# A Flamingo block on one core: row tables, means and gathers around the choice of experts

## What is computed

```
x = x + tanh(g_xattn[0]) * cross_attention(layernorm(x), ctx)         # 77 keys
x = x + tanh(g_ffn[0])   * quantised_gated_ffn(layernorm(x))
x = x + tanh(g_xattn[1]) * attention_16_heads(layernorm(x), ctx)
x = x + tanh(g_ffn[1])   * experts(layernorm(x))

def experts(x):                                   # 2048 tokens
    logits = (x @ w_red) @ (wg / norm(wg)).T      # 8 experts
    gates = softmax(logits);  idx = argmax(gates);  score = max(gates)
    h = gelu(x @ W1[idx] + b1[idx])               # 256 -> 512
    return (h @ W2[idx] + b2[idx]) * score        # 512 -> 256
```

## Time and profile before

| | us |
|---|---|
| median of 3 runs | 446.13 (445.56 to 446.71) |
| the profiled execution | 443.87 |
| its span | 442.1 |
| PE, DVE, ACT, POOL busy | 402.4, 314.8, 252.8, 133.8 |
| mean granted clock of TensorE | 0.947 of 2.4 GHz |

### The profile page before, as it was taken

The page is one execution under the profiler, slowest core; times in us unless marked ns, Lnnn a source line. Parts: engine busy times, 40 slices in busy tenths (PEclk is TensorE's granted clock), DMA queues, the critical chain, the costliest instruction groups (busy, mean ns, idle before and its releaser), DMA issues.

```text
span 442.1 us, 8460 instructions
## 1 busy us (share of the span) xinstructions
PE 402.4 (91%) x2922; PEld 305.0 (69%) x2923; DVE 314.8 (71%) x662; ACT 252.8 (57%) x423; POOL 133.8 (30%) x159
## 2 busy tenths in 40 slices
PE   8998899999997906999999999999996999999992
PEld 7887744444444606888886777777685589999991
DVE  3999985449999998886487799988876344444442
ACT  3563556559999893551358777887832433443320
POOL 6614145200000072231119700020127745552221
PEclk9999999999999555999999999999999799999997
DMA  7920000000002000500049920002221847666600
GB/s 245 307 5 0 1 3 0 0 0 0 0 0 64 2 0 0 116 0 0 1 154 394 397 12 3 2 1 98 93 76 54 292 150 215 208 211 171 170 22 0
DMA packets 37813, 38.34 MB, mean 87 GB/s; under 512 B 16620, under 2 KB 28595, under 8 KB 37524
## 3 DMA queue, kind: packets, MB, share of 16 engines
q1 hardware_dynamic: 35571, 32.76, 24.3%
q0 software_dynamic: 2208, 5.14, 3.5%
HBM read 33.66 MB, written 5.15 MB: 88 GB/s over the span
## 4 chain that ended last, share of the span: by engine, by line
PE 65%; DVE 9%; ACT 6%; POOL 3%; issue 3%; DMA 2%; DVEq 0%; ACTq 0%; POOLq 0%
PE quad L1760 30%; PE bank L1760 27%; PE bank L2083 4%; ACT tmp L965 2%; ACT big_u L960 1%; DMA big_u<-token_rows,k_blockdiag 1%; ACT big_u L812 1%; DVE amZ L1356 1%; DVE amU L1362 1%; DVE mx L1578 1%; PE bank L2120 1%; DVE big_g L1576 1%; PE quad L1804 1%; POOL big_g L782 1%; POOL big_u L782 1%
## 5 line engine op out<-in xcount | busy, mean ns | idle before, releaser
L1760 PE MATMUL quad<-yT,ffn_w 128*128 (+1 forms) x128 | 56.3, 593 | 0.0
L812 ACT ACTIVATE big_u<-bank 77x512 f32<-77x512 f32 (+2 forms) x72 | 38.9, 589 | 11.8 <-PE bank L2083 10.6
L1760 PEld LDWEIGHTS quad<-yT,ffn_w 128*128 128x128 f32 x128 | 24.0, 190 | 29.5 <-issue 28.3
L1760 PE MATMUL bank<-big_u,yT 128*128 x184 | 43.6, 380 | 0.5 <-issue 0.5
L1760 PEld LDWEIGHTS quad<-yT,x_rows 128*128 128x128 f32 x336 | 40.7, 192 | 1.0
L1760 PE MATMUL quad<-yT,x_rows 128*128 128x128 f32 x336 | 40.9, 275 | 0.0
L789 POOL DMA_INDIRECT out<-yT,k_blockdiag x23 | 23.0, 1001 | 46.5 <-DVE yT L1728 45.7
L1760 PEld LDWEIGHTS bank<-big_u,yT 128*128 128x128 f32 x184 | 33.2, 190 | 4.7 <-issue 1.1
L1712 DVE TENSOR_TENSOR yT<-quad,tmp 128x512 f32<-128x512 f32 x21 | 14.5, 691 | 28.7 <-PE quad L1760 28.7
L812 ACT ACTIVATE yT<-quad 128x256 f32<-128x256 f32 x23 | 8.7, 382 | 40.3 <-PE quad L1804 40.2
L1760 PE MATMUL quad<-ffn_w,big_u 128*128 128x256 f32 x144 | 31.5, 380 | 0.1
(11 more groups left out here) (350 smaller groups left out, 913.3 us busy)
## 6 DMA issues: line engine op xcount, KB each, us to landing
x_rows<-in_L_ffn_W SPq DMA_DIRECT2D x21, 512.0 KB, 3.8
big_g<-in_L_ffn_W SPq DMA_DIRECT2D x1, 4096.0 KB, 14.5
big_u<-in_L_ffn_W SPq DMA_DIRECT2D x1, 4096.0 KB, 25.0
x_rows<-in_x SPq DMA_DIRECT2D x4, 512.0 KB, 6.5
ffn_w<-in_L_ffn_b SPq DMA_DIRECT2D x1, 2048.0 KB, 25.0
tmp<-bias_by_distance SPq DMA_DIRECT2D x2, 616.0 KB, 5.8
token_rows<-x_rows SPq DMA_DIRECT2D x1, 1032.0 KB, 5.4
tmp<-in_L_ffn_b SPq DMA_DIRECT2D x1, 1024.0 KB, 5.5
```

The costliest lines, as they stand in the source:

```text
L812: act.activation(out_, in_, ACT.Copy, **k).then_inc(done, 1)
L1760: return pe.matmul(out_, lhsT=lhsT, rhs=rhs, start=first, stop=last)
```

## The change

1. **Row tables.** AT_ROW is made ahead of PLACE, tile by tile: eleven tiles by VectorE with a tensor_scalar of 128 columns each, five by ScalarE as 1 - (place - rem)^2, cut at 0 (three squares and one difference, then two and one). PE waits for PLACE and all of VectorE's tables first.
2. **Small matmuls.** PE's counting of tiles 14 and 15 stands between the two halves of tile 14's projection. VectorE's counting moves ahead of the residual of tile 14, the residual of tile 15 behind two steps of the positions.
3. **Last rows.** The means of the last tiles are computed one by one, each on its own wait; the power is written straight into X, without the copy.
4. **Gathers.** AHEAD is 8 instead of 12, the groups are 1, 1, 2, 2, 2, 4, 4, 4 and 3.
5. **Idle matmuls.** 12 + 11 become 19 ahead of the placing matmuls, 16 become 18 behind them, three new ones stand between the transposes of the first two slots.
6. Four semaphores of VectorE become one that it raises four times.

```diff
-GATHERS = (1, 1, 2, 4, 4, 4, 4, 3)
-AHEAD = 12
+GATHERS = (1, 1, 2, 2, 2, 4, 4, 4, 3)
+AHEAD = 8
...
+        BY_DVE = 11
...
             def last_rows_ready(k):
                 b, e = ROW_PARTS[2 + k]
-                pool.wait_ge(s.x3_done, e)
-                pool.tensor_scalar(nmean[:, k, :], xsum[:, k, :], -1.0 / D, None, ALU.mult).then_inc(s.nmean_sb, 1)
+                for u in range(2):
+                    pool.wait_ge(s.x3_done, b + u + 1)
+                    pool.tensor_scalar(nmean[:, k, u:u + 1], xsum[:, k, u:u + 1], -1.0 / D, None,
+                                       ALU.mult).then_inc(s.nmean_sb, 1)
                 pool.wait_ge(s.dev_sb, 2 * k + 2)
                 c.link(pool.tensor_scalar(ve4[:, b:e], xdev[:, k, :], 1.0 / D, EPS, ALU.mult, ALU.add))
-                c.link(pool.tensor_tensor(rstd4[:, b:e], ve4[:, b:e], mhalf[:, b:e], ALU.pow))
-                pool.tensor_copy(X[:, b:e, RSTD], rstd4[:, b:e])
...
+                c.link(pool.tensor_tensor(X[:, b:e, RSTD], ve4[:, b:e], mhalf[:, b:e], ALU.pow))
...
             squares(1)
+            act.wait_ge(s.rem_sb, 1)
+            for n, (t, e) in enumerate(((BY_DVE, BY_DVE + 3), (BY_DVE + 3, NT))):
+                for u in range(e - t):
+                    ins = act.activation(apart[:, n, u, :], lane[:, :], ACT.Square, scale=-1.0, bias=rem[:, t + u:t + u + 1])
+                c.link(ins)
+                act.activation(AT_ROW[:, t:e, :], apart[:, n, 0:e - t, :], ACT.Relu, scale=-1.0,
+                               bias=ones[:, 0:1]).then_inc(s.at_row_a, 1)
             act.wait_ge(s.lxs_sb, 1)
...
+            for t in range(BY_DVE):
+                dve.tensor_scalar(AT_ROW[:, t, :], lane[:, :], rem[:, t:t + 1], None, ALU.is_equal).then_inc(s.at_row_sb, 1)
...
-            for g in range(NT // 4):
-                dve.tensor_tensor(AT_ROW[:, 4 * g:4 * g + 4, :], lane[:, :].unsqueeze(1).to_broadcast([P, 4, P]),
-                                  rem[:, 4 * g:4 * g + 4].unsqueeze(2).to_broadcast([P, 4, P]),
-                                  ALU.is_equal).then_inc(s.at_row_sb, 1)
...
-                project(t, 0)
-                counts(t, NT)
+                project(t, 0, lambda: counts(t, NT))
                 project(t, 1)
-                idle_work(pb[2], 12)
...
-            idle_work(pb[2], 11)
+            idle_work(pb[2], 19)
...
-            idle_work(pb[2], 16)
+            idle_work(pb[2], 18)
...
-            for u in range(2):
-                inputs(u, 0)
+            inputs(0, 0)
+            idle_work(pb[2], 3)
+            inputs(1, 0)
```

More of the change, by code:

```diff
@@ L178, in __init__ @@
         self.nmean_sb = sem("nmean_sb")
+        self.rem_sb = sem("rem_sb")
+        self.at_row_a = sem("at_row_a")
         self.dev_sb = sem("dev_sb")
@@ L436, in flamingo_kernel @@
         nmean = sb("x3_nmean", [P, 2, 2])
+        apart = part(TMP, 5632, [P, 2, 3, P], F16)
         LM = sb("lm", [P, NT])
@@ L1286, in _ @@
             dve.wait_ge(s.els_sb, 1)
-            dve.tensor_scalar(hscale[:, :], els[:, :], 4.0, HD ** -0.5, ALU.min, ALU.mult).then_inc(s.hsc_sb, 1)
+            dve.tensor_scalar(hscale[:, :], els[:, :], 4.0, HD ** -0.5, ALU.min, ALU.mult).then_inc(s.l1_prep_sb, 1)
             c.link(dve.tensor_tensor(wg2[:, :], wg[:, :], wg[:, :], ALU.mult))
@@ L1292, in _ @@
             dve.tensor_scalar(bo1c[:, :], bo1c[:, :], tg[:, 1:2], None, ALU.mult)
-            dve.tensor_scalar(bo1[:, :], bo1[:, :], tg[:, 1:2], None, ALU.mult).then_inc(s.wo_sb, 1)
+            dve.tensor_scalar(bo1[:, :], bo1[:, :], tg[:, 1:2], None, ALU.mult).then_inc(s.l1_prep_sb, 1)
             dve.wait_ge(s.wnorm_sb, 1)
@@ L1297, in _ @@
             c.link(dve.reciprocal(wss[:, 2:3], wss[:, 1:2]))
-            dve.tensor_scalar(wgn[:, :], wg[:, :], wss[:, 2:3], None, ALU.mult).then_inc(s.wgn_sb, 1)
+            dve.tensor_scalar(wgn[:, :], wg[:, :], wss[:, 2:3], None, ALU.mult).then_inc(s.l1_prep_sb, 1)
             dve.tensor_scalar(keepv[:, :], keepc8[:, :], -1.0, 1.0, ALU.mult, ALU.add)
@@ L1645, in _ @@
             gate(LAST, NT)
-            residual(LAST, 0)
             dve.wait_ge(s.cnt_ps, 1)
@@ L1653, in _ @@
             c.link(dve.tensor_reduce(start_e[:, :], earlier[:, :, :], AX.X, ALU.add))
-            residual(LAST, 1)
+            residual(LAST, 0)
             c.link(dve.scalar_tensor_tensor(CUM, start_e[:, :].unsqueeze(1).to_broadcast([P, NT, E]), float(P),
@@ L1658, in _ @@
             c.link(dve.tensor_tensor(CUM, CUM, OHB[:, :, :], ALU.mult))
+            residual(LAST, 1)
             c.link(dve.tensor_reduce(LM[:, :], CUM, AX.X, ALU.add))
@@ L1661, in _ @@
             c.link(dve.tensor_scalar(pos_i[:, :], pos_i[:, :], 7, None, ALU.arith_shift_right))
-            c.link(dve.scalar_tensor_tensor(rem[:, :], pos_i[:, :], -float(P), LM[:, :], ALU.mult, ALU.add))
+            dve.scalar_tensor_tensor(rem[:, :], pos_i[:, :], -float(P), LM[:, :], ALU.mult, ALU.add).then_inc(s.rem_sb, 1)
+            dve.wait_ge(s.rem_sb, 1)
+            for t in range(BY_DVE):
+                dve.tensor_scalar(AT_ROW[:, t, :], lane[:, :], rem[:, t:t + 1], None, ALU.is_equal).then_inc(s.at_row_sb, 1)
             c.link(dve.tensor_tensor(IN_SLOT, nth[:, :].unsqueeze(1).to_broadcast([P, NT, NS]),
@@ L2130, in project_in, with project @@
                 ins.then_inc(s.attT_ps, 2)
-            def project(t, u):
+            def project(t, u, between=None):
                 if u == 0:
@@ L2137, in project @@
                 for ci in range(CH):
+                    if ci and between is not None:
+                        between()
                     ins = mm(pb[5 - u if t == LAST else 4][:, u * D:(u + 1) * D], attT[:, u, ci * P:(ci + 1) * P], WO1[:, ci, :],
@@ L2247, in _ @@
             last_tiles()
-            idle_work(pb[2], 11)
+            idle_work(pb[2], 19)
             pe.wait_ge(s.place_sb, 1)
+            pe.wait_ge(s.at_row_sb, BY_DVE)
             for t in range(NT):
-                pe.wait_ge(s.at_row_sb, t // 4 + 1)
+                if t == BY_DVE:
+                    pe.wait_ge(s.at_row_a, 1)
+                if t == BY_DVE + 3:
+                    pe.wait_ge(s.at_row_a, 2)
                 ins = mm(pb[7][:, 0:NS], AT_ROW[:, t, :], PLACE[:, t, :], t == 0, t == NT - 1)
             ins.then_inc(s.owner_ps, 1)
-            idle_work(pb[2], 16)
+            idle_work(pb[2], 18)
             pe.wait_ge(s.slots_sb, 1)
```

30 lines of the change are left out of this document (14 added, 16 removed).

## The result

The changed kernel takes **454.25 us** (median, 453.75 to 455.56), the kernel before 446.25 us in the same comparison: 1.0186 of it, 95% interval 1.0168 to 1.0205. It is slower, as forecast, 3.3 us above the forecast of 450.9 and inside the range. Its profiled execution took 454.6 us, the span 452.8, 10.7 more than the 442.1 of before. The median rose by less, 8.0 us: the profiled execution of before lay 2.3 us under its median, that of the changed kernel 0.35 us over it.

A forecast was written before the change was run, and what follows sets the result against it. Before the loop the path of rows to the first gather decides, in the loop PE. Span 442.1 - 4.8 (front) + 7.5 (stalls) + 2.1 (clock) = 446.9 us, carried over to a median of 450.9 us; range 445 to 456.

The forecast's parts named there:

- The stalls: Loop: PE waits at slots 8, 12 and 16 for a group's last gather, 2.5 us each, +7.5 us (4.5 to 10.6).
- The clock: Loop: after a stall PE may go on at 1.2 GHz; one fall in three taken, +2.1 us (0 to 6.3).
- The absorbed case: Loop: gather 11 issues by 365.8, PE notices no wait; worth 7.5 and 2.1, median 441.3 us; 12 in 100.
- The small-stalls rival: Loop: each gather lands in the row's shortest time, no clock fall, stalls 4.5 us, median 445.8 us; 15 in 100.
- First gather: Before the loop, on GpSimd: starts at 335.5 instead of 336.89, 1.4 us earlier (0.8 to 1.9).
- Indices: Before the first gather: ready at 334.1 to 335.6, until now 335.1, with the row path still deciding.
- Second gather: Before the loop, on GpSimd: 1.93 us beside VectorE's table of shares gets 0.6 us shorter (0 to 0.9).
- (f): Before the loop: idle matmuls shrink PE's gaps; if its clock stays at 2.4 GHz, 2.1 us gained (0 to 2.1).
- (g): Before the loop: PE's third wait, 0.68 us for the eighth gather, goes with the smaller group: 0.7 us (0 to 0.7).

The follow-up runs named there:

- e1: The changed kernel with the gather plan of before (twelve ahead, groups 1,1,2,4,4,4,4,3): 0.9968 of the kernel before.
- e2: The kernel before with only the gather plan changed (eight ahead, groups 1,1,2,2,2,4,4,4,3): 451.2 us, 1.0152 of the kernel before.
- e3: The changed kernel with nine gathers ahead instead of eight, groups unchanged: 441.46 us, 0.9947 of the kernel before.
- e4: The changed kernel, still eight ahead, with groups 1,1,2,4,2,2,4,4,3: 450.0 us, 1.0134 of the kernel before.
- f3: The changed kernel with nine ahead and the row tables of before (four of 128x512 on VectorE behind the places): 440.7 to 440.9 us.
- f2: The changed kernel with nine ahead and the idle matmuls of before: 440.7 to 440.9 us.
- g1: The changed kernel with nine ahead, run once more as common reference: 440.95 us, 0.9929 of the kernel before.
- f1: The changed kernel with nine ahead, weight loads of slots 2 to 5 held until gathers 2 to 5 have landed: 444.5 us.
- g3: The changed kernel with nine ahead, only weight loads of slots 4 and 5 held until gathers 2 to 5 have landed: 439.1 us, 0.9918 of before.
- g4: Nine ahead, loads of slots 4 and 5 held for gathers 2 to 5, those of slots 2 and 3 behind gather 0 alone: 442.55 us.
- f4: The changed kernel with nine ahead and the last rows' means as before (one mean for two tiles, the copy kept): 440.7 to 440.9 us.

## Why the prediction was right, point by point

- **The stalls** came at slots 8, 12 and 16 and nowhere else, for the reason given: e1 and e2 move them with the gather plan, e3 removes them with one gather more, e4 removes the one whose group is split. The term was mis-sized: 9.4 us against 7.5 (the forecast's own numbers, 373.57 less 371.16, give 2.4 each, 7.2 in all). The first stall is 3.6 instead of 2.5, because the result of slot 3 waited for a store and the gather behind it went out 1.7 us later than the row of before said; where that wait didn't occur (e2) it is 2.6. From that gather's issue to the normalisation it is only 3.1 us (367.65 to 370.72), where 3.8 was taken; at the two other stalls it is 4.0 and 4.2, hence their 2.8 and 3.0.
- **The clock** fell behind two of the three gaps, 1.7 and 1.8 us, where one in three was taken at 2.1. That it was two, and not one or three, is luck as far as the forecast goes: the forecast has nothing that tells which gap brings the clock down.
- **The absorbed case** was put at an issue of gather 11 2.5 us earlier. It is what nine ahead makes of it, with 0.6 us to spare. The small-stalls rival failed on the late result at the first stall and on the landing at the others.
- **The number.** Part of the hit is luck. The forecast of the span was 446.9 us and it became 452.8, 5.9 more; the median was missed by only 3.3, because the 2.3 us by which the profile of before lay under its median were carried over, and the profile after didn't lie under its own.
- **First gather:** 1.45 us earlier from A, forecast 1.4. Two errors cancel. GpSimd kept its quick pace, 1.35 us, so the rows were ready 1.9 us earlier; but from there to the gather it took 3.3 us (333.05 to 336.32) and not 2.86. By the rule from the Trainium skill that was set beside it ("VectorE: DVE Perf Modes", perf-mode tier table, with "GPSIMD Engine Reference", Key points) the tables would have disturbed GpSimd as the old ones did. The trace doesn't agree for these tensor_scalar of 128x128 in 16 bits: 1.35 us beside them, against 1.28 for the same three operations on tiles 12 and 13, ahead of them (325.72 to 327.00); whether they ran in the two-port mode, no row shows. For two-input tables it does agree: 2.22 us in f3, and 2.97 for four operations before.
- **Indices:** there at 335.39, or 334.5 on the clock of before, inside 334.1 to 335.6, and not deciding, as said. The tables took 0.17 us each.
- **Second gather:** 0.95 us, all of the 0.9 that were possible; slot 1's transposes started 2.5 us earlier from A (forecast 2.0). The second gather was over (338.87) before the table of shares began (338.91), which now slowed the third gather to 1.87 us; the forecast had not asked what the table would meet next.
- **The step that failed is (f), with (g).** The clock stayed up and the first layer got 2.0 us shorter, as said. That it shows at the start of the loop was wrong: behind it the fourth gather was next late, and PE waited 1.09 us. f2, where the clock falls there, has slot 0's second layer at 24.43 us from A, between e3 and g1: no price of the clock shows at that point. The wait for slot 4 stayed, 0.60 of 0.68. So the front is worth 3.2 us and not 4.8, part of it by the smaller early groups: e2, with the old front, has 2.2 of it (two profiles of one kernel, e3 and g1, differ by 1.1 in this stretch, so the split is rough).

## What to carry to other kernels

A prefetch distance is measured to the last transfer that the first use of a group waits for: eight ahead with groups of four is five ahead, and one more can be the whole difference. When a stall or a slow clock is taken away, follow each later wait of that engine to its own producer before the gain is counted; here the gathers and the weight loads shared the DMA engines (0.98 busy from 344 to 346 us), and holding all loads back until the gathers had landed made PE wait 4.68 us for weights (f1). Read the engine's order before a load is held: only in g3, where the loads held weren't needed next, did slot 0's second layer come earlier, and that this shortens the whole kernel isn't shown.

## What the runs showed of the hardware that was not expected

- A gap's length did not decide whether PE's clock fell: behind gaps of 2.58 and 1.83 us at the transposes it fell, behind 1.98 it didn't (changed kernel); 1.66 and 1.80 fell, 1.71 didn't (e2); 1.81 and 1.83 both didn't (e4). Ahead of the loop the same: behind 1.85 (e4, slot 4), 1.76 (g4) and 2.03 (e1, both slot 2) it fell, behind 1.84 (g1, slot 2) it didn't. What does decide wasn't found out.
- A gather on GpSimd takes 0.95 to 1.3 us, and up to 1.93 when it starts while VectorE's table of shares (a two-input operation, 1.31 us) runs. It then ends 0.82 us behind the table's end: issued 0.20 us into the table it takes 1.93 us (before), at 0.26 us 1.87 (changed), at 1.01 us 1.12 (f3), at 1.12 us 1.01 (e2, f4). A gather that starts ahead of the table is not slowed, though the two overlap by 0.7 to 0.8 us (0.95 us in e2, f3 and f4). The rows look like a wait for the table's end and not like slower work beside it.
- The kernel before differed by up to 2.9 us from one chip to another, more than most of the edits here, while nine ahead with the new front, or with its idle work, tables or means undone, stayed between 440.7 and 441.5. The two with the whole front ran in other sets than the three with a part undone, so chip and edit can't be told apart here. Why the one moves and the others don't stays open.
